# Attention weights in four transfers, sequence 0's mixes and sequence 1's scalings moved forward, decays read as a broadcast column

## The reference

```python
xx = q_shift_1d(x)                      # half of the channels shifted by one token
xk = x * mix_k + xx * (1 - mix_k)       # the same with mix_v and mix_r
k, v, r = xk @ Wk.T, xv @ Wv.T, xr @ Wr.T
# scan over tokens, ew = exp(decay / T), eku = exp(first / T + k), ek = exp(k)
out = (a + eku * v) / (b + eku)         # then a = a * ew + ek * v, b = b * ew + ek
x = layernorm(x + (sigmoid(r) * out) @ Wo.T)
...
x = layernorm(x + selected_block(x))
```

## Time and profile before

| | |
|---|---|
| median of 3 runs | 781.01 us (780.63 to 783.65) |
| profiled execution | 784.69 us, span 783.0 us |
| PE busy | 741.6 us, 95% |
| DVE, ACT, POOL busy | 647.7, 516.2, 511.7 us |
| mean granted TensorE clock | 0.965 of full |

### The profile page before, as it was taken

How to read it: one execution, slowest core, us unless ns; L and a number is a source line. 1 busy time by engine, 2 the same in 40 slices (tenths; PEclk the granted TensorE clock), 3 DMA queues, 4 the chain that set the end, 5 groups by cost and what they waited for, 6 DMA issues and landing times. The chain is left out here.

```text
span 783.0 us, 13078 instructions
## 1 busy us (share of the span) xinstructions
PE 741.6 (95%) x4390; PEld 550.7 (70%) x4390; DVE 647.7 (83%) x1324; ACT 516.2 (66%) x983; POOL 511.7 (65%) x495
## 2 busy tenths in 40 slices
PE   7899999999999999999988999999999999999993
PEld 5466666666666666666556576777788777899993
DVE  6698998989989899899999987679956677568784
ACT  2677888888888888878766774757555766632120
POOL 1587887878878788787767667746737683532323
PEclk8999999999999999999999998979989999999998
DMA  8012524233242332422322211224001120000001
GB/s 231 5 40 61 155 68 134 67 106 95 67 134 69 108 94 73 130 68 88 113 68 68 68 47 36 90 81 141 16 14 48 49 82 2 1 2 28 28 15 41
DMA packets 37337, 55.40 MB, mean 71 GB/s; under 512 B 3360, under 2 KB 26528, under 8 KB 37280
## 3 DMA queue, kind: packets, MB, share of 16 engines
q1 hardware_dynamic: 34464, 46.28, 19.6%
q0 software_dynamic: 2816, 8.39, 3.6%
HBM read 35.78 MB, written 18.87 MB: 70 GB/s over the span
## 5 line engine op out<-in xcount | busy, mean ns | idle before, releaser
L793 PE MATMUL ps<-halves 128*128 128x512 f32 x558 | 239.1, 537 | 0.0
L788 PE MATMUL ps<-arena,wa 128*128 128x512 f32 x384 | 206.3, 620 | 15.6 <-DVE arena L1576 6.8
L793 PEld LDWEIGHTS ps<-halves 128*128 128x128 f32 x558 | 107.7, 193 | 100.6 <-issue 92.1
L808 PE MATMUL ps<-wa,arena 128*128 128x256 f32 x512 | 131.7, 380 | 0.0
L594 POOL TENSOR_TENSOR arena<-arena 128x1024 f32<-128x1024 f32 x32 | 76.2, 2382 | 79.7 <-issue 56.3
L578 POOL TENSOR_TENSOR arena<-arena 128x512 f32<-128x512 f32 x93 | 116.5, 1285 | 6.4 <-ACT halves L1200 6.4
L788 PEld LDWEIGHTS ps<-arena,wa 128*128 128x128 f32 x384 | 71.4, 194 | 45.3 <-POOL halves L579 14.2
L1544 DVE TENSOR_TENSOR_SCAN arena<-ewb,ps 128x511 f32<-128x511 f32 x64 | 74.5, 1206 | 30.6 <-ACT ps L1172 29.7
L808 PEld LDWEIGHTS ps<-wa,arena 128*128 128x128 f32 x512 | 87.3, 190 | 6.6
L585 POOL TENSOR_TENSOR arena<-arena 128x1024 f32<-128x1024 f32 x32 | 76.3, 2383 | 22.5 <-ACT arena L1186 22.5
L1571 DVE TENSOR_TENSOR_SCAN arena<-ewb,ps 128x511 f32<-128x511 f32 x64 | 74.1, 1200 | 0.0
(11 more groups left out here) (231 smaller groups left out, 1522.4 us busy)
## 6 DMA issues: line engine op xcount, KB each, us to landing
arena<-x_chan SPq DMA_DIRECT2D x32, 512.0 KB, 4.3
out<-arena SPq DMA_DIRECT2D x32, 512.0 KB, 3.2
arena<-x_chan SPq DMA_DIRECT2D x64, 127.8 KB, 3.4
wa<-w_attn SPq DMA_DIRECT2D x1, 1024.0 KB, 7.9
wa<-w_up SPq DMA_DIRECT2D x1, 1024.0 KB, 5.7
wa<-w_down SPq DMA_DIRECT2D x1, 1024.0 KB, 5.3
wqk<-w_qk SPq DMA_DIRECT2D x1, 512.0 KB, 5.2
wv<-w_v SPq DMA_DIRECT2D x1, 256.0 KB, 5.5
```

The costliest lines, as they stand in the source:

```text
L788: mm(bank[:, o, :], wa[:, m, 0, out_part], xm[s.par][:, m, :], start=True, stop=False)
L793: last = mm(bank[:, o, :], w[:, m, out_part], x[s.par], start=False, stop=(t == 2))
L808: last = mm(psY[:, j, :], gg[s.par][:, c, tokens], wa[:, 3, c, :], start=False, stop=(c == CC - 1))
```

## The change

`wa` comes in four transfers, each with a semaphore, the K, V and R matrices directly behind sequence 0's channels and O behind sequence 1's; `cols` has a semaphore of its own, and `rwb`, `rbb` and `ptok` move back in SP's order. DVE does sequence 0's difference and mixes before the rotary angles. ACT's scalings(1) stand ahead of exp_k(0). On DVE num(0) stands ahead of clamp(0), for sequence 0 alone. `ewb` is no longer filled (its space, now `shifted`, only serves a later stage): the scans read `euw`'s column with a step of zero. The fillers go from 18 to 21.

```diff
-            sp.dma_start(cols[:, :], columns).then_inc(small_in, 16)
-            sp.dma_start(rwb[:, :], router_w.rearrange("(a c) -> a c", a=1).to_broadcast([P, C])).then_inc(small_in, 16)
-            sp.dma_start(rbb[:, :], router_b.rearrange("(a c) -> a c", a=1).to_broadcast([P, 1])).then_inc(small_in, 16)
...
+            def load_weight(m):
+                sp.dma_start(wa[:, m, :, :], w_attn[m].rearrange("(c p) o -> p c o", p=P)).then_inc(w_in[m], 16)
+            sp.dma_start(cols[:, :], columns).then_inc(cols_in, 16)
+            load_channels(At(0, 0))
+            for m in range(3):
+                load_weight(m)
             sp.dma_start(ptok[:, :], positions).then_inc(pos_in, 16)
-            load_channels(At(0, 0))
-            sp.dma_start(wa[:, :, :, :], w_attn.rearrange("m (c p) o -> p m c o", p=P)).then_inc(w_in, 16)
             load_channels(At(0, 1))
+            sp.dma_start(rwb[:, :], router_w.rearrange("(a c) -> a c", a=1).to_broadcast([P, C])).then_inc(small_in, 16)
+            sp.dma_start(rbb[:, :], router_b.rearrange("(a c) -> a c", a=1).to_broadcast([P, 1])).then_inc(small_in, 16)
+            load_weight(3)
             for k in range(RING):
                 period(At(0, k))
             for dst, src in ((wqk, w_qk), (wv, w_v), (wo, w_o)):
...
+                    if is_start(s):
+                        pe.wait_ge(w_in[m], 16)
...
+                if is_start(s):
+                    pe.wait_ge(w_in[3], 16)
...
-            keep_warm(7, 18)
-            pe.wait_ge(w_in, 16)
+            keep_warm(7, 21)
...
-            act.wait_ge(small_in, 3 * 16)
+            act.wait_ge(cols_in, 16)
             a.activation(euw[:, :, :], uw, ACT.Exp, scale=1.0 / T).then_inc(eu_made, 1)
             act.wait_ge(consts_made, 4)
-            act.wait_ge(w_in, 16)
+            for m in range(3):
+                act.wait_ge(w_in[m], 16)
             a.activation(w1_hi, wa[:, 0:3, 1, :], ACT.Copy).then_inc(w1_rounded, 1)
             def exp_k_of(s):
...
+                if is_start(at):
+                    differences_scaled(at.back(-1))
                 if at.exists():
                     exp_k_of(at)
                 if at.had(1) and at.back(1).exists():
                     reciprocal_of(at.back(1))
-                if at.back(-1).exists():
+                if at.back(-1).exists() and not is_start(at):
...
+            dve.wait_ge(cols_in, 16)
+            dve.wait_ge(chan_in[0], 48)
+            v.tensor_tensor(diff[:, :], xc[0][:, 0, :], xs[0][:, :], ALU.subtract).then_inc(diff_made, 1)
+            dve.wait_ge(diff_made, 1)
+            for m, done in enumerate((None, scaled, mixed)):
+                last = v.scalar_tensor_tensor(xm[0][:, m, :], diff[:, :], mix[:, m:m + 1], xs[0][:, :], ALU.mult, ALU.add)
+                if done is not None:
+                    last.then_inc(done, 1)
...
-                    last = v.tensor_tensor_scan(bb[:, c, 1:T], ewb[:, c, 0:T - 1], psK[:, c, 0:T - 1], 0.0, ALU.mult, ALU.add)
+                    last = v.tensor_tensor_scan(bb[:, c, 1:T], euw[:, 1, c:c + 1].to_broadcast([P, T - 1]), psK[:, c, 0:T - 1], 0.0, ALU.mult, ALU.add)
...
                     products_of(at)
-                    clamp_of(at)
-                    num_of(at)
+                    if is_start(at):
+                        num_of(at)
+                        clamp_of(at)
+                    else:
+                        clamp_of(at)
+                        num_of(at)
                 if isinstance(at.n, int):
                     selection(at.n)
                 if at.had(1) and at.back(1).exists():
```

More of the change, by code:

```diff
@@ L80, in rwkv_then_selected_block_kernel @@
         euw = sb("euw", [P, 2, CC])
-        ewb = sb("ewb", [P, CC, T])
+        shifted = sb("shifted", [P, CC, T])
         rwb = sb("rwb", [P, C])
@@ L231, in rwkv_then_selected_block_kernel @@
         kblk = [place(CC, 2 * P) for _ in range(2)]
-        sc = ewb.rearrange("p a (h k) -> p (a h) k", k=K)
+        sc = shifted.rearrange("p a (h k) -> p (a h) k", k=K)
         pT = both(H // 2, P)
@@ L262, in rwkv_then_selected_block_kernel @@
         row_out = [sem(f"row_out{p}") for p in range(4)]
-        w_in = sem("w_in")
+        w_in = [sem(f"w_in{m}") for m in range(4)]
         w2_in = sem("w2_in")
+        cols_in = sem("cols_in")
         small_in = sem("small_in")
@@ L269, in rwkv_then_selected_block_kernel @@
         eu_made = sem("eu_made")
-        ewb_made = sem("ewb_made")
         rw_chain = sem("rw_chain")
@@ L451, in tables_of, with is_start @@
             return 2 if 2 * first + 1 < MB else 1
+        def is_start(at):
+            return isinstance(at.n, int) and at.n == 0
         def pair(n):
@@ L564, in _ @@
             pool.wait_ge(consts_made, 4)
-            pool.wait_ge(small_in, 3 * 16)
             def differences_of(s):
@@ L1486, in _ @@
             v.tensor_scalar(trn, trt, PI, -PI, ALU.min, ALU.max).then_inc(ang_ready, 1)
[L1488 to L1497, removed]
             dve.wait_ge(iotas_made, 3)
@@ L1522, in _ @@
             v.reduce_sum(bm[:, :], blk[:, :].rearrange("p (n h) -> p h n", h=2), AX.X).then_inc(bm_made, 1)
-            for c in range(CC):
-                v.tensor_scalar(ewb[:, c, :], ewb[:, c, :], euw[:, 1, c:c + 1], None, ALU.mult).then_inc(ewb_made, 1)
+            dve.wait_ge(small_in, 2 * 16)
             v.bn_stats(rwst[:, 0:6], rwb[:, :]).then_inc(rw_chain, 1)
@@ L1530, in _ @@
             dve.wait_ge(rw_chain, 3)
-            dve.wait_ge(ewb_made, 1 + CC)
             dve.wait_ge(first_col, 2)
@@ L1570, in num_of @@
                 for c in range(CC):
-                    v.tensor_tensor_scan(aa[:, c, 1:T], ewb[:, c, 0:T - 1], psV[:, c, 0:T - 1], 0.0, ALU.mult, ALU.add).then_inc(scan_a_done, 1)
+                    v.tensor_tensor_scan(aa[:, c, 1:T], euw[:, 1, c:c + 1].to_broadcast([P, T - 1]), psV[:, c, 0:T - 1], 0.0, ALU.mult, ALU.add).then_inc(scan_a_done, 1)
                 if s.had(2):
```

## The result

The changed kernel takes 783.97 us, median of 20 runs (781.67 to 786.38); the kernel before, measured beside it in 20 runs, takes 782.06 us (778.47 to 786.26). The ratio is 1.0037 with a 95% interval of 1.0021 to 1.0053: slower by 2.9 us (1.6 to 4.1), where the forecast was 1.2 us faster. The medians differ by 1.9 us. The 20 runs of before spread over 7.8 us, those of after over 4.7, and the fastest of before is 3.2 us under the fastest of after, while the slowest differ by 0.1 us. The profiled executions taken alone say the opposite: a span of 782.1 us after, 783.0 before.

A forecast was written before the change was run, and what follows sets the result against it. A loop over ACT, POOL and PE (13.95 us a turn) was taken to bound the kernel, its end moving with K(2)'s start, set by gate(0). 781.01 - 1.2 = 779.8 us; range 776.6 to 782.6.

The forecast's parts named there:

- its times are used for differences only: Profiled execution of before, 784.69 us and 3.7 above the median: only differences between its times enter the forecast.
- PE's lead is spent on ACT's queue: Sequence 0: PE's 4.9 us lead is lost as K(0) waits 5 us for ACT; exp_k(0) at 18.85 or 19.35.
- The late clamp holds ln_gate(0), exp_k(1) and gate(0): Clamp behind num(0) on DVE ends at 30.4, not about 28.0; ln_gate(0) starts then, exp_k(1) at 31.4.
- The gate at 35.15: POOL's gate(0), after sum(0) and difference 2, starts at 35.15 instead of 36.32.
- the term of 1.2 us: K(2) starts at 42.5 instead of 43.70 and the loop keeps that: 1.2 us earlier.
- The scans cost nothing: DVE's 128 scans with a zero-step column: 0 to 0.01 us more each, at most 0.4 us in the last ten sequences.
- the clock falls in the new pause: Rival, 17%: PE's 1.9 us pause ahead of outputs(0) brings the low clock; 781.5 within 780.7 to 782.2.
- PE's lead passes through: Rival, 17%: K(1)'s 3.6 us lead stays, giving 777.4, or all of R(0)'s 4.9 us, giving 776.1.
- late data: Rival, 7%: `ptok` landing after 10.4 delays angles through exp_k(0) one for one; at 12.4 the time is 781.8.
- the zero step's rival: Rival, 4%: each zero-step scan is dearer; at 0.24 us more, the last ten sequences cost 9.6 us: 788.2.
- K(1)'s 4.93 us: PE's K(1), assumed at low clock as before: 4.93 us, from 28.22 to 33.18 in the old trace.
- What the end keeps: Loop over ACT, POOL and PE, 13.95 us a turn: the end moves with the start of K(2).

The follow-up runs named there:

- angles-first kernel: Changed kernel with positions loaded right behind the columns and the angles ahead of sequence 0's difference and mixes on DVE; ratio to before 1.0002.
- two traces of before: The kernel before, unedited, traced twice: executions of 784.69 and 779.68 us; ratio of before to itself 1.0003.
- zero-step kernel: Kernel before with only its den and num scans reading a column with step zero, the tile still filled; ratio to before 1.0021.
- second trace of after: The changed kernel, unedited, timed and traced once more; ratio to before 1.0048.

## Why the prediction was wrong

The step that failed is the base of the comparison: "its times are used for differences only". The difference was taken between a path over ACT and DVE that hardly varies, and one execution of a path over PE that does. K(2) of before at 43.70 was the latest of three: 43.70, 40.58, 39.00 (the last with the zero-step scans), with granted clocks of 0.78, 0.91 and 1.00 over the same 18 us. The changed kernel's was at 43.98, 44.49 and 44.08 (the last with fillers). The means are 41.1 and 44.2, and their difference of 3.1 us is the measured 2.9 within its interval, though three executions a side are few. Of the 4.1 us between forecast (1.2 faster) and result (2.9 slower), some 2.6 are this base (43.70 against 41.1), and 1.5 a term of the sum that is named below. The sign that was missed is in the prediction's own text: the profiled execution was 3.7 us above the median, and K(0) and K(1) were seen at low clock.

Point by point. *PE's lead is spent on ACT's queue*: right. K(0) started at 9.64 (10.4 forecast) and exp_k(0) at 19.89 (18.85). *The late clamp holds ln_gate(0), exp_k(1) and gate(0)*: right, and taking it away gave K(2) at 41.42. *The gate at 35.15*: 1.3 us too early. `ptok` came at 10.7 and not 10.4. The channels of sequence 1 came at 12.78 and not from 14.2 on, so POOL's difference met the angles, which took 1.0 us longer beside it; the sum had no term for that. The rec(0) waits for sum(0), which the sum left out (0.71 us of wait at 35.16), though POOL's difference 2 covered most of it. So K(2) came 0.28 us after the old trace's, not 1.2 before: the term of 1.2 us was mis-sized by 1.5, of which 1.0 is DVE's wait for POOL.

*The scans cost nothing*: right, 1205 and 1199 ns; the 0.35 us that the prediction estimated from the Trainium skill's rule on runs of adjacent words (Vector Engine (DVE) Microarchitecture Reference, section 5.2) are not seen for a step of zero. The rival *the clock falls in the new pause* did not come about: the pause was 1.18 us, and the clock stayed at 1.00 from 38 to 42 us; in the angles-first kernel, with 1.97 us, it fell. The rival *PE's lead passes through* did not come about either, and *late data* was worth 0.3 us. Two figures of the prediction are off without moving its forecast: the 788.2 of the zero step's rival should be 789.4 (779.8 and 9.6), and K(1)'s 4.93 us are 4.96.

*What the end keeps*: right for the loop. The 3.15 us between the two traces of before stand almost unchanged from rec(0) to the rec near 440 us (438.78 and 435.63), and in all fourteen traces rec(28) starts 394.9 to 395.2 us after K(2). Behind it the executions differ again, with other stretches at the low clock: from rec(28) to the end it takes between 339.7 and 345.9 us, 344.2 and 342.3 in the two traces of before. So one execution's time does not show what its start was worth, and only the medians do. By these the other kernels follow K(2), nearly: those with traces at 36.9 to 39.3 have ratios of 0.996 to 0.998, those at 41.0 to 41.8 of 1.000 to 1.002, those at 43.1 to 44.5 of 1.003 to 1.007; the zero-step kernel, which starts as before does, has 39.00 in its one trace and 1.0021.

## What to carry to other kernels

Before a term is subtracted from a trace, ask whether its start varies: a stretch behind a pause of PE can run at 1.2 or 2.4 GHz in two executions of one program, and the profile shows one of them. When data arrives earlier, look at what else is queued on the engine that must act on it next; here the late sine, the table load, the weights' rounding and the scalings on ACT used up all of it. An order that lets one consumer start earlier (num ahead of the clamp, for V(1)) delays the other, and the other's queue decides what that costs. A test with fillers is one only if they end before the work that they are to speed up could start: 34 of them raised K(1)'s clock and put off its start by as much as it gained.

## What the runs showed of the hardware

An instruction of DVE can wait for a whole one of POOL. In the second trace of after DVE's rows around POOL's difference 1 (13.63 to 15.02) read:

```profile
13.47 0.42 DVE L1506 SCALAR_TENSOR_TENSOR arena<-arena 128x256 f32<-128x256 f32 x1
13.93 1.18 DVE L1507 TENSOR_SCALAR arena<-arena 128x128 f32<-128x128 f32 x1
15.14 0.30 DVE L1508 TENSOR_SCALAR arena<-arena 128x256 f32<-128x256 f32 x1
```

L1506 started first and kept its 0.42 us; L1507, which takes 0.23 us in the first trace, took 1.18 and ended with POOL's instruction. In the first trace L1506 was the one that waited. The Trainium skill, SBUF — State Buffer, section "Who interferes with whom", says that DVE and GpSimd share a pair of SBUF ports as an exclusive lock for a whole instruction; both traces agree, 0.95 to 1.0 us each time. Not every pair does this: DVE's L1568, with one input in PSUM, took 1.41 us beside POOL's L587 in the first trace (24.19 against 23.72 to 24.98), and its twin L1586 1.38 with POOL idle.

A pause of the same 2.55 or 2.56 us ahead of K(1) was followed by the low clock in one trace of before and by the full clock in two others (the second trace and that of the zero-step scans); a pause of 1.97 us ahead of outputs(0) was followed by the low clock in the angles-first trace. The Trainium skill, TensorE: Matmul & The Clock Gate, Part 1, says that the number of slow matmuls at a kernel's start varies from run to run; the three traces of before's start agree, with 6.40, 5.42 and 3.74 us from K(0) to exp_k(0).
